# An attention and mixture-of-experts kernel: all queue lists laid out anew, and the idle products taken out

## The chip, the core and the metric

The kernel runs on one core of a Trainium2 chip. The metric is the device time of one execution in microseconds. The kernel before took 829.53 us (median of 3 runs, 828.97 to 829.89).

## The reference, cut to what matters

32 sequences (here called tiles) of 128 tokens with 256 features each go through two blocks. Everything is fp32.

```
A (cross-attention), 16 heads of 16:
  q = layernorm(x) Wq' + bq;  k, v = ctx Wk' + bk, ctx Wv' + bv
  x = x + tanh(g_xattn) * (softmax(where(mask, -1e9, q k' / 4)) v Wo' + bo)
B (causal self-attention and experts) on y = layernorm(x):
  q, k from rope(y), v from y; causal softmax; attn_out with out_proj
  u = layernorm(y + attn_out) * ln1_w + ln1_b
  gates = softmax(u gate_w' + gate_b); the two largest of 8 experts are kept
  moe = sum over the chosen experts of gate * (u expert_w' + expert_b)
  x = x + tanh(g_ffn) * (layernorm(u + moe) * ln2_w + ln2_b)
```

## The kernel before, in words

A tile is 128 tokens by 256 features. Weights stay in SBUF, each as a high and a low part (`w_Aka`, `w_Akb` and so on); a product of fp32 accuracy is three products of the parts, high by high, high by low and low by high (`products`, L391 to L396). A part is made by ScalarE (`split_high`, L746; a copy) and VectorE (`split_low`, L929; a subtraction). Activations are split in the same way (`high_part`, L752, L758, on ScalarE; `low_part`, L967, L974, on VectorE).

Eight banks of PSUM are used: four score banks hold the 16 heads' 128 by 128 scores, and four work banks hold everything else. Which use takes which work bank, and in which turn, is written out in `WORK_USES`; `take_work` (L386) makes TensorE wait for the reader of the use before.

One attention of one tile goes through the score banks thus:

1. ScalarE seeds the four banks with the mask (`seed_scores`, L765, L776; 4 instructions).
2. TensorE adds the scores, query by key (`scores`, L505, 16 products at L516).
3. VectorE takes the negative maxima, bank by bank (`maxima`, L1017, L1022; 4 instructions), and `max_parts` (L1026) makes a bf16 high and low part of them, four copies of 2 x 16 columns.
4. For A, ScalarE seeds the banks with the transposed mask (`seed_scores_t`, L779, L785). TensorE writes the scores again, key by query (`scores_t`, L521, 32 products at L535).
5. TensorE transposes the maxima (`transpose_max`, L546), ScalarE copies them out (`max_transposed`, L818), and TensorE adds them with `pick`, a table with a row for each of 16 heads (`subtract_max`, L556, 16 products).
6. ScalarE takes the exponentials (`exponentials`, L826; 4 instructions); for B, GpSimd zeroes what is not causal (`causal`, L1343). TensorE multiplies by the values (`attend`, L574); ScalarE copies the result to `o_raw` (`raw_values`, L834), one buffer for A and B.

Then follow a transposition (L585), the division by the sums (VectorE), another transposition, the split, and the output projection (`project_o`). Around this stand the norms: VectorE has statistics (L952, L960) and the scaling (L964), GpSimd the inverse root (`inverse_root`, L1260, L1263). GpSimd also splits the context (`context_parts`, L1271, L1273) and widens the mask (`mask_of_tile`, L1280). It waits for a tile's context and mask with one semaphore, `ld_c`.

**The order of the work** is written out by hand. Each engine has a list, run once for each round r, and each entry names its own tile by an offset, as `scores("A", 2 * r - 1)`. An entry whose tile does not exist is left out (`live`). A round has two tiles, and each queue is strictly in order, so the lists are the schedule: TensorE L627 to L741, ScalarE L858, VectorE L1141, GpSimd L1389, and SyncE, which only issues transfers, L342 to L382. In TensorE's list A runs two tiles ahead of B and five ahead of the experts (`expert_pair`, L613). A tile's k and q projections are made for two tiles together (`project_pair`, L455).

In the first rounds and the last ones few entries are live. There `keep_busy` (L407) issues products of the identity that nobody reads:

```python
            def keep_busy(use, t, count):
                bank = take_work(use, t)
                for _ in range(count):
                    pe.matmul(bank[:], ident_bf[:], ident_bf[:].unsqueeze(1).to_broadcast([P, GROUP, P]), start=True, stop=True)
```

SyncE's list before the rounds loads tiles 0 and 1 first, then Ak, Av, tile 2's x and context, Aq, small rows, tile 3, and so on. The rows of the norms, the gates and the expert biases (11 transfers) come behind.

## Time and profile before

| What | before |
|---|---|
| median of 3 runs | 829.53 us (828.97 to 829.89) |
| span of the profiled execution | 829.5 us |
| TensorE busy | 779.7 us (94%) |
| VectorE busy | 667.5 us (80%) |
| ScalarE busy | 564.4 us (68%) |
| GpSimd busy | 473.0 us (57%) |
| products of `keep_busy` | 167 |

The profile gives the time from the first to the last instruction (the span), and for each engine the time in which one of its instructions ran. A busy TensorE is not TensorE at its peak, since products overlap and their ends are modelled; the time from one start to the next says more. "Idle before, releaser" is the time that an engine had nothing to run, and the instruction that ended it. PEclk is the granted TensorE clock as a share of 2.4 GHz.

### The profile page before, as it was taken

The numbers are of one execution on the slowest core, as the hardware profiler recorded it, in microseconds if no ns is written. First come the engines' busy times: TensorE is split into PE (matmuls) and PEld (weight loads), VectorE is DVE, ScalarE is ACT, GpSimd is POOL, SyncE is SP. The second block draws the span as 40 slices with busy tenths as digits, with TensorE's granted clock in tenths as the row PEclk, the third lists the DMA queues.
The fourth block names the chain that finished last, engine by engine and source line by source line (L and its number), as shares of the span: only waits on it lengthen the run. The fifth ranks groups of instructions, "written<-read, shape, count | busy, mean of one in ns | idle before, by whom it ended". The sixth has DMA issues, their size and how long they took to land.

```text
span 829.5 us, 24325 instructions
## 1 busy us (share of the span) xinstructions
PE 779.7 (94%) x9515; PEld 611.9 (74%) x9515; DVE 667.5 (80%) x1908; ACT 564.4 (68%) x1268; POOL 473.0 (57%) x854
## 2 busy tenths in 40 slices
PE   8888989999999999999999999999999999999896
PEld 4465768777787787778787788778778777777663
DVE  5756668797978979797988979797988979787876
ACT  5786767777786777777776777678677777764320
POOL 8434535566665646566574646566564655555343
PEclk9999999999999999999999999999999999999999
DMA  7510000010100101010100101010010000000000
GB/s 202 159 39 16 2 17 16 8 37 9 37 8 2 37 8 36 9 36 9 29 16 2 38 8 37 8 37 9 10 35 2 9 8 8 9 8 8 8 7 20
DMA packets 33570, 20.75 MB, mean 25 GB/s; under 512 B 11672, under 2 KB 33456, under 8 KB 33456
## 3 DMA queue, kind: packets, MB, share of 16 engines
q1 hardware_dynamic: 33456, 19.19, 8.1%
q8 instruction: 76, 1.25, 0.6%
q14 instruction: 38, 0.31, 0.1%
HBM read 14.99 MB, written 4.19 MB: 23 GB/s over the span
## 4 chain that ended last, share of the span: by engine, by line
PE 56%; ACT 24%; DVE 14%; issue 4%; POOL 1%; DMA 0%; SPq 0%; DVEq 0%; POOLq 0%
PE bank L395 26%; PE bank L516 8%; PE bank L535 7%; ACT bank L776 6%; DVE neg_max_A L1022 6%; ACT bank L785 5%; DVE moe L1131 4%; ACT probs_B L826 3%; PE bank L556 3%; PE bank L585 3%; ACT probs_A L826 3%; PE bank L574 2%; PE bank L404 2%; ACT k_heads_B L809 2%; PE bank L546 1%
## 5 line engine op out<-in xcount | busy, mean ns | idle before, releaser
L1343 POOL TENSOR_SCALAR_AFFINE_SELECT probs_B<-probs_B 128x512 f32<-128x512 f32 x128 | 77.3, 640 | 184.4 <-ACT probs_B L826 184.4
L1131 DVE SCALAR_TENSOR_TENSOR moe<-bank,gates,moe 128x256 f32<-128x256 f32 x256 | 123.2, 481 | 48.2 <-PE bank L395 33.2
L785 ACT ACTIVATE bank<-mask_add 128x512 f32<-128x512 bf16 x128 | 76.6, 602 | 49.2 <-DVE neg_max_A L1022 49.2
L395 PE MATMUL bank<-w_expertsa,u_t_a 128*128 128x512 f32 x256 | 105.6, 413 | 0.1
L395 PE MATMUL bank<-w_expertsa,u_t_b 128*128 128x512 f32 x256 | 100.9, 394 | 0.0
L395 PE MATMUL bank<-w_expertsb,u_t_a 128*128 128x512 f32 x256 | 100.9, 394 | 0.0
L1022 DVE TENSOR_REDUCE neg_max_A<-bank 128x4 f32<-128x512 f32 x128 | 79.5, 684 | 11.9 <-PE bank L516 11.5
L1022 DVE TENSOR_REDUCE neg_max_B<-bank 128x4 f32<-128x512 f32 x128 | 79.3, 682 | 5.5 <-PE bank L516 5.5
L776 ACT ACTIVATE bank<-mask_add 128x512 f32<-128x512 bf16 x128 | 69.8, 626 | 0.0
L776 ACT ACTIVATE bank<-causal_add 128x512 f32<-128x512 bf16 x128 | 69.7, 623 | 0.0
L826 ACT ACTIVATE probs_A<-bank 128x512 f32<-128x512 f32 x128 | 66.1, 603 | 4.4 <-PE bank L556 2.2
L826 ACT ACTIVATE probs_B<-bank 128x512 f32<-128x512 f32 x128 | 66.2, 607 | 3.2 <-PE bank L556 1.1
L834 ACT ACTIVATE o_raw<-bank 128x512 f32<-128x512 f32 x64 | 38.5, 602 | 27.8 <-PE bank L574 27.8
L395 PEld LDWEIGHTS bank<-w_expertsa,u_t_a 128*128 128x128 f32 x256 | 49.1, 192 | 10.6 <-issue 0.4
L1260 POOL TENSOR_SCALAR var_eps<-mean_var 128x1 f32<-128x1 f32 x64 | 12.3, 192 | 77.7 <-DVE mean_var L960 75.2
L395 PEld LDWEIGHTS bank<-w_expertsa,u_t_b 128*128 128x128 f32 x256 | 48.1, 188 | 11.4
L395 PEld LDWEIGHTS bank<-w_expertsb,u_t_a 128*128 128x128 f32 x256 | 48.3, 189 | 6.7
L535 PEld LDWEIGHTS bank<-q_heads_A,k_heads_A 32*128 32x128 f32 x1024 | 31.4, 186 | 22.4 <-ACT bank L785 22.4
L809 ACT ACTIVATE k_heads_A<-bank,k_cols_A,head_rows 128x256 f32<-128x256 f32 x64 | 30.9, 565 | 23.0 <-PE bank L395 23.0
L535 PE MATMUL bank<-q_heads_A,k_heads_A 32*128 32x128 f32 x1024 | 37.5, 283 | 8.1 <-ACT bank L785 7.4
L411 PE MATMUL bank<-ident_bf 128*128 128x512 bf16 x167 | 42.7, 396 | 1.9 <-ACT k_heads_B L809 1.9
L516 PE MATMUL bank<-k_heads_A,q_heads_A 32*128 32x256 f32 x512 | 36.7, 399 | 5.8 <-ACT bank L776 4.7
(224 smaller groups left out, 2440.5 us busy)
## 6 DMA issues: line engine op xcount, KB each, us to landing
x_in<-in_x SPq DMA_DIRECT2D x32, 128.0 KB, 2.2
ctx_t<-in_ctxT SPq DMA_DIRECT2D x32, 128.0 KB, 2.2
out<-y_out SPq DMA_DIRECT2D x32, 128.0 KB, 1.7
w_stage<-in_expertsT SPq DMA_DIRECT2D x8, 256.0 KB, 4.3
mask_u<-in_masks SPq DMA_DIRECT2D x32, 32.0 KB, 2.1
w_stage<-in_in_projT SPq DMA_DIRECT2D x3, 256.0 KB, 4.8
w_stage<-in_WkT SPq DMA_DIRECT2D x1, 256.0 KB, 3.5
w_stage<-in_WvT SPq DMA_DIRECT2D x1, 256.0 KB, 3.6
```

The costliest lines, as they stand in the source:

```text
L395: done = pe.matmul(out_ap, l, r, start=n == 0, stop=n == len(terms) - 1)
L411: pe.matmul(bank[:], ident_bf[:], ident_bf[:].unsqueeze(1).to_broadcast([P, GROUP, P]), start=True, stop=True)
L516: done = pe.matmul(score_banks[g][:, c * 2 * P:(c + 1) * 2 * P], queries[strip, half, c, :], keys[strip, half, c, :, :], start=False, stop ...
L535: pe.matmul(score_banks[g][:, i * P:(i + 1) * P], keys[strip, half, c, odd, :], queries[strip, half, c, :], start=tag == "B" and i == 0, s ...
L776: act.activation(score_banks[g][:].rearrange("p (h k) -> p h k", k=P), mask[:, 0:1, :].to_broadcast([P, GROUP, P]), ACT.Copy).then_inc(sem ...
L785: act.activation(score_banks[g][:].rearrange("p (h k) -> p h k", k=P), mask_add[t % MASK_SLOTS][:, 1:2, :].to_broadcast([P, GROUP, P]), AC ...
L809: act.activation(k_heads[tag][pair % PAIR_SLOTS][:, :, c, odd, :], bank[:, c * PAIR * P:(c + 1) * PAIR * P].rearrange("p (j n) -> p j n", ...
L826: act.activation(probs[tag][:, g * GROUP:(g + 1) * GROUP, :].rearrange("p h q -> p (h q)"), score_banks[g][:], ACT.Exp, scale=SCALE).then_ ...
L834: act.activation(o_raw[:], work_bank(tag + "_values", t)[:], ACT.Copy).then_inc(sem[tag + "_or"], 1)
L1022: dve.tensor_reduce(neg_max[tag][:, g * GROUP:(g + 1) * GROUP], score_banks[g][:].rearrange("p (h k) -> p h k", k=P), AXIS_X, ALU.max, neg ...
L1131: dve.scalar_tensor_tensor(out=moe[(e + 1) % 2][:], in0=bank[:, (e % 2) * EMBED:(e % 2 + 1) * EMBED], scalar=gates[:, e:e + 1], in1=moe[e ...
L1343: pool.affine_select(out=part, in_=part, compare_op=ALU.is_ge, fill=0.0, base=0, pattern=[[0, GROUP], [1, P]], channel_multiplier=-1).then ...
```

## The change

- `PIECES = 4`: what was a loop over four score banks is now a list entry for each piece of one bank. `scores` and `subtract_max` increment their semaphore once, behind the last product, where they did it four times; `scores_t` now increments one.
- Every engine's list and `WORK_USES` are new. A still runs two tiles ahead of B and five ahead of the experts.
- SyncE's list before the rounds is gone: each transfer stands in a round.
- All `keep_busy` entries are gone.
- `pick` has 4 columns of rows instead of 16 (`GROUP` instead of `HEADS`), is made by VectorE from the identity, and `max_parts` writes each head's maximum once, 16 columns per part where it was 64. GpSimd's `make_picks` (a memset and two selects of 128x2048) goes.
- `o_raw` has a buffer for A and one for B. Some waits that another wait implies go, others are added.

```diff
-        pick = sb("pick", [P, HEADS, P], BF16)
+        pick = sb("pick", [P, GROUP, P], BF16)
+        strip_rows = sb("strip_rows", [P, GROUP])
-        o_raw = sb("o_raw", [P, BANK])
+        o_raw = {t: sb(f"o_raw_{t}", [P, BANK]) for t in "AB"}
+        def score_piece(c):
+            return scores_ps[:, c * PIECE_BANKS:(c + 1) * PIECE_BANKS, :].rearrange("p g (h k) -> p (g h) k", k=P)
...
-                        if c == CHUNKS - 1:
-                            done.then_inc(sem[tag + "_s"], 1)
+                done.then_inc(sem[tag + "_s"], 1)
...
-                hi, lo = copies[:, :, 0:HEADS], copies[:, :, HEADS:2 * HEADS]
-                whole = neg_max[tag][:].unsqueeze(1).to_broadcast([P, GROUPS, HEADS])
+                hi, lo = copies[:, :, 0:GROUP], copies[:, :, GROUP:2 * GROUP]
+                whole = neg_max[tag][:].rearrange("p (g n) -> p g n", n=GROUP)
...
+            def exponentials(tag, c, t):
+                if not live(t):
+                    return
+                act.wait_ge(sem[tag + "_sm"], t + 1)
+                act.activation(probs[tag][:, c * PIECE_HEADS:(c + 1) * PIECE_HEADS, :], score_piece(c), ACT.Exp,
+                               scale=SCALE).then_inc(sem[tag + "_exp"], 1)
```

SyncE's new list, with its waits inside `load_weight` and `load_tile` as before:

```python
            for r in rounds:
                store(2 * r - 30)
                if r == 13: load_weight("E2")
                if r == 11: load_weight("E1")
                load_tile(2 * r - 19)
                if r == 10: load_weight("Bk")
                if r == 1:  load_weight("Ao"); load_row(bo_A)
                store(2 * r - 29)
                if r == 1:  load_weight("Ak")
                if r == 13: load_weight("E7")
                if r == 10: load_weight("Bq"); rope_cos, rope_sin, bv_B
                if r == 3:  load_weight("Av")
                if r == 14: load_weight("E6")
                if r == 11: load_weight("Bv")
                if r == 10: load_weight("Bo"); bo_B, ln1_w, ln1_b, ln2_w, ln2_b, gate_bias, bias_f x3, gate_f
                if r == 12: load_weight("E5"); load_weight("E3")
                load_tile(2 * r - 18)
                if r == 12: load_weight("E4")
                if r == 11: load_weight("E0")
                if r == 0:  load_weight("Aq"); head_rows, bias_cols, two gains, bv_A
```

TensorE's new list (each line in the order of the list):

```
transpose_max B 2r-5, o_transposed A 2r-3, y_transposed 2r-5, subtract_max B 2r-5, normalise B 2r-6,
project_o A 2r-3, project_v_a 2r-2, project_v_b 2r-5, gate 2r-7, o_transposed B 2r-6, rope_transposed 2r-4,
x_t 2r, scores A 2r-2, attend B 2r-5, rope_transposed 2r-3, project_o B 2r-6, normalise B 2r-5,
project_k_b r-2, transpose_max A 2r-2, scores_t A 2r-2, subtract_max A 2r-2, expert_pair 0 2r-7,
transpose_gates 2r-7, project_q_b r-2, expert_bias_sum 2r-7, expert_pair 1 and 2 2r-7, scores B 2r-4,
attend A 2r-2, o_transposed B 2r-5, y_transposed 2r-4, expert_pair 3 2r-7, u_transposed 2r-6,
scores_t B 2r-4, transpose_max B 2r-4, normalise A 2r-2, subtract_max B 2r-4, gate 2r-6, project_v_b 2r-4,
o_transposed A 2r-2, project_o B 2r-5, expert_pair 0 2r-6, project_v_a 2r-1, project_o A 2r-2,
transpose_gates 2r-6, scores A 2r-1, attend B 2r-4, expert_bias_sum 2r-6, expert_pair 1 2r-6, x_t 2r+1,
transpose_max A 2r-1, scores_t A 2r-1, subtract_max A 2r-1, expert_pair 2 and 3 2r-6, project_k_a r,
scores B 2r-3, attend A 2r-1, project_q_a r, normalise A 2r-1, u_transposed 2r-5, scores_t B 2r-3
```

The stretches of the other lists that the prediction speaks of:

```
ScalarE: ... seed_scores A pieces 2, 3 2r-9, gates_transposed 2r-14, seed_scores_t 0 2r-9, raw_values B 2r-12,
  seed_scores_t 1, 2, 3 2r-9, max_transposed A 2r-9, high_x 2r-7, exponentials A 0, 1, 2 2r-9, seed_scores B 0, 1 2r-11, ...
  keep_keys A r-4, raw_values A 2r-9, keep_queries A r-4, ... seed_scores A 0 to 3 2r-8 ...
  (in ScalarE's list 2r-9 is the odd tile of A, 2r-1 in TensorE's, and 2r-12 the even tile of B, 2r-4 in TensorE's)
VectorE: ... statistics A 2r-1, statistics 2, low_o A, apply_x 2r-2, ... add_values A 2r-4, ... low_x 2r-2,
  maxima A 0, 1, 2 2r-4, low_rope 2r-5, maxima A 3 2r-4, max_parts A 2r-4 ...
GpSimd:  scale_shift_u 2r-12, base_a 2r-8, causal 0 to 2, context_parts 2r-4, causal 3, inverse_root 2, base_a 2r-7,
  mask_of_tile 2r-6, inverse_root 1, inverse_root B, rope, ... inverse_root A 2r-4, ... mask_of_tile 2r-5, ...
```

## Rows read from the trace of the kernel before

**Rows 1.** Windows over two stretches: start and end, length, busy us of PE, PEld, DVE, ACT, POOL, PEclk.

```profile
16.20:118.80 102.60, 89.88 (x1142) 62.19 (x1142) 63.91 (x147) 74.52 (x159) 46.39 (x84) 1.00 0.20 57
118.80:731.90 613.10, 593.78 (x7594) 482.00 (x7594) 524.10 (x1530) 448.75 (x1017) 367.13 (x666) 1.00 0.06 17
```

**Rows 2.** Timeline of PE over one round: start, length, line, operation, idle before.

```profile
353.25 1.08 PE L574 MATMUL bank<-probs_B,values_B 128*32 128x128 f32 x32
354.61 1.15 PE L516 MATMUL bank<-k_heads_A,q_heads_A 32*128 32x256 f32 x16 [0.27 <-ACT bank L776]
...
371.14 1.17 PE L535 MATMUL bank<-q_heads_B,k_heads_B 32*128 32x128 f32 x32
372.25 0.23 PE L546 MATMUL bank<-ident_bf,neg_max_bf_B 128*128 128x128 bf16 x1
...
378.46 1.15 PE L516 MATMUL bank<-k_heads_A,q_heads_A 32*128 32x256 f32 x16
379.53 1.08 PE L574 MATMUL bank<-probs_B,values_B 128*32 128x128 f32 x32
...
381.94 0.40 PE L395 MATMUL bank<-w_expertsa,u_t_b 128*128 128x512 f32 x1
382.79 1.17 PE L535 MATMUL bank<-q_heads_A,k_heads_A 32*128 32x128 f32 x32 [0.46 <-ACT bank L785]
```

**Rows 3.** Timeline of PE, the start of the next round.

```profile
401.76 0.50 PE L516 MATMUL bank<-k_heads_A,q_heads_A 32*128 32x256 f32 x4 [0.28 <-ACT bank L776]
```

**Rows 4.** Timelines of DVE and ACT in the same round.

```profile
379.62 2.48 DVE L1022 TENSOR_REDUCE neg_max_A<-bank 128x4 f32<-128x512 f32 x4 [0.46 <-PE bank L516]
382.48 0.18 DVE L1034 CAST neg_max_bf_A<-neg_max_A 128x64 bf16<-128x64 f32 x1
...
380.35 2.39 ACT L785 ACTIVATE bank<-mask_add 128x512 f32<-128x512 bf16 x4 [1.50 <-DVE neg_max_A L1022]
382.68 0.58 ACT L834 ACTIVATE o_raw<-bank 128x512 f32<-128x512 f32 x1
...
397.50 2.07 ACT L826 ACTIVATE probs_B<-bank 128x512 f32<-128x512 f32 x4
399.43 2.18 ACT L776 ACTIVATE bank<-mask_add 128x512 f32<-128x512 bf16 x4
```

**Rows 5.** Timeline of SP, the transfers' issues.

```profile
0.79 0.37 SPq L313 DMA_DIRECT2D x_in<-in_x  x1
...
17.68 1.09 SPq L309 DMA_DIRECT2D gate_bias<-in_L_ffn_gate_b  x1
...
21.35 1.23 SPq L313 DMA_DIRECT2D x_in<-in_x  x1
```

**Rows 6.** Timelines of POOL and ACT, the first instructions behind a transfer.

```profile
4.14 0.40 POOL L1271 CAST ctx_ab_a<-ctx_t 128x256 fp32r<-128x256 f32 x1 [1.79 <-DMA mask_u<-in_masks]
4.62 0.73 POOL L1273 TENSOR_TENSOR ctx_ab_b<-ctx_t,ctx_ab_a 128x256 fp32r<-128x256 f32 x1
...
9.50 0.63 ACT L750 ACTIVATE w_Aqa<-w_stage 128x512 fp32r<-128x512 f32 x1 [0.75 <-DMA w_stage<-in_WqT]
```

**Rows 7.** Timeline of PE, the scores of A for tiles 0 and 1.

```profile
16.19 1.15 PE L516 MATMUL bank<-k_heads_A,q_heads_A 32*128 32x256 f32 x16 [0.27 <-ACT q_heads_A L795]
31.27 1.15 PE L516 MATMUL bank<-k_heads_A,q_heads_A 32*128 32x256 f32 x16 [0.38 <-ACT bank L776]
```

**Rows 8.** Timeline of PE, the scores of B for tiles 30 and 31.

```profile
765.45 1.15 PE L516 MATMUL bank<-k_heads_B,q_heads_B 32*128 32x256 f32 x16
783.84 1.15 PE L516 MATMUL bank<-k_heads_B,q_heads_B 32*128 32x256 f32 x16
```

**Rows 9.** PE where the clock fell: a window of 3.4 us, and a group of 32 products in it.

```profile
748.10:751.50 3.40, 3.40 (x54) 2.64 (x50) 2.43 (x14) 1.55 (x6) 0.00 (x0) 0.50 0.00 0
...
747.85 1.93 PE L535 MATMUL bank<-q_heads_B,k_heads_B 32*128 32x128 f32 x32 [1.27 <-DVE neg_max_B L1022]
```

**Rows 10.** Window of PE, products of `keep_busy` (L411) alone: length, busy us of PE, of PEld.

```profile
16.20:118.80 102.60, 25.88 (x108) 9.68 (x108) 1.00 0.20 57
```

More of the change, by code:

```diff
@@ L534, in scores_t @@
                             i = 2 * c + odd
[L535 to L537 removed]
+                            done = pe.matmul(scores_ps[:, g, i * P:(i + 1) * P], keys[strip, half, c, odd, :],
+                                             queries[strip, half, c, :], start=tag == "B" and i == 0, stop=False,
+                                             skip_group_check=True)
+                done.then_inc(sem[tag + "_st"], 1)
             def transpose_max(tag, t):
@@ new lines, in tensor_program @@
+                project_o("A", 2 * r - 3)
+                project_v_a(2 * r - 2)
+                project_v_b(2 * r - 5)
+                gate(2 * r - 7)
+                o_transposed("B", 2 * r - 6)
+                rope_transposed(2 * r - 4)
+                x_t(2 * r)
+                scores("A", 2 * r - 2)
+                attend("B", 2 * r - 5)
+                rope_transposed(2 * r - 3)
+                project_o("B", 2 * r - 6)
+                normalise("B", 2 * r - 5)
+                project_k_b(r - 2)
@@ new lines, in tensor_program @@
+                transpose_max("A", 2 * r - 2)
+                scores_t("A", 2 * r - 2)
+                subtract_max("A", 2 * r - 2)
+                expert_pair(0, 2 * r - 7)
+                transpose_gates(2 * r - 7)
+                project_q_b(r - 2)
+                expert_bias_sum(2 * r - 7)
+                expert_pair(1, 2 * r - 7)
+                expert_pair(2, 2 * r - 7)
+                scores("B", 2 * r - 4)
+                attend("A", 2 * r - 2)
+                o_transposed("B", 2 * r - 5)
@@ L628, in tensor_program @@
+                y_transposed(2 * r - 4)
+                expert_pair(3, 2 * r - 7)
+                u_transposed(2 * r - 6)
+                scores_t("B", 2 * r - 4)
+                transpose_max("B", 2 * r - 4)
+                normalise("A", 2 * r - 2)
+                subtract_max("B", 2 * r - 4)
                 gate(2 * r - 6)
                 project_v_b(2 * r - 4)
-                if r == 1:
-                    keep_busy("x_t", 2, 3)
+                o_transposed("A", 2 * r - 2)
+                project_o("B", 2 * r - 5)
@@ L650, in tensor_program @@
-                scores_t("A", 2 * r - 1)
-                transpose_max("A", 2 * r - 1)
-                rope_transposed(2 * r - 2)
-                subtract_max("A", 2 * r - 1)
-                normalise("B", 2 * r - 4)
                 expert_pair(3, 2 * r - 6)
-                o_transposed("B", 2 * r - 4)
-                if r == 1:
-                    keep_busy("A_v", 2, 4)
+                project_k_a(r)
+                scores("B", 2 * r - 3)
                 attend("A", 2 * r - 1)
+                project_q_a(r)
@@ L726, in tensor_program @@
-                y_transposed(2 * r - 2)
-                scores("B", 2 * r - 2)
-                if r == 0:
-                    keep_busy("x_t", 2, 4)
-                attend("A", 2 * r)
-                o_transposed("B", 2 * r - 3)
-                project_v_a(2 * r + 1)
-                normalise("A", 2 * r)
-                if r == 16:
-                    keep_busy("B_values", 30, 9)
-                scores_t("B", 2 * r - 2)
-                transpose_max("B", 2 * r - 2)
-                if r == 0:
-                    keep_busy("x_t", 2, 5)
@@ L1299, in rope, with keep @@
                 pool.tensor_tensor(roped[:], roped[:], rope_tmp[:], ALU.add).then_inc(sem["rope3"], 1)
+            def keep(t):
+                if not live(t):
+                    return
+                if t == 0:
+                    pool.wait_ge(sem["c_fold_2"], 2)
+                kept = x1[t % X1_SLOTS]
+                pool.tensor_tensor(kept[:], kept[:], rows["ln2_b"][:], ALU.add).then_inc(sem["kept"], 1)
             def finish(t):
```

1031 lines of the change are left out of this document (535 added, 496 removed).

## The prediction

> **What bounds the kernel now.** I read the windows by stage first. From tile 5's scores of A at 118.8 us to tile 31's at 731.9 TensorE is busy for 593.78 of 613.10 us [rows 1]; no other engine comes near. These are 26 tiles or 13 rounds, so a round is 47.16 us; two starts of the same entry, 354.61 and 401.76, give 47.15 [rows 2, 3]. Around this steady stage stand a fill of 118.8 us and a drain of 829.5 - 731.9 = 97.6 us. Of the fill, 16.2 us pass before the first scores [rows 7], 102.6 us between them and the sixth.
>
> The timeline shows what TensorE's steady round still loses. The ends of its products are modelled, so I take start to start. An entry that waits for nothing starts just before the modelled end of the one ahead (378.46 + 1.15 = 379.61, next start 379.53) [rows 2]. Against that 353.25 + 1.08 leads to a start at 354.61 (about 0.35 us late, the seeds), and the last expert product, started at 381.94 and usually 0.23 apart, is followed by `scores_t` only at 382.79: 0.85 us, 0.64 of it lost, again to ScalarE's seeds [rows 2]. Both bounds of the whole loss: the empty time is (613.10 - 593.78) / 13 = 1.5 us a round [rows 1]; summing every late start in the round as above I get 2.5. So the round can fall to 44.65 us at the best, and nothing but other waits decides where it lands: the products in it are the same ones. That is worth at most 2.5 x 13 = 32 us.
>
> The sum is made against the span of the profiled execution, 829.5 us, which is the median of the runs too. About 0.2% (1.7 us) is what a measurement of this kernel can tell from no change.
>
> **Part 1, the steady round: -13 us.** Pieces of one bank are the same instructions as before, of the same 512 columns; they cost nothing and only let other work stand between them. I walk through the new lists with the lengths of before. The cycle of the score banks is: scores 1.15, maxima 2.4, one more seed 0.6, `scores_t` 1.17, subtraction, four exponentials 1.93, four seeds 2.1 [rows 2, 4].
>
> - Odd tile of A: TensorE puts attend B, the bias, one expert pair and `x_t` between `scores` and `scores_t`, about 4.0 us. ScalarE's chain is: scores and first maximum 1.95, seed 0.6, then `raw_values` B 0.55, which now stands between pieces 0 and 1, then three seeds 1.8: 5.05 us [rows 4]. A wait of 1.05 us, where before it was 0.64. This is the largest that I find.
> - `transpose_max` A now stands ahead of `scores_t`. At the even tile 5.2 us of work cover it; then ScalarE's copy of the maxima hides behind `scores_t` and the subtraction no longer waits. This takes away some 0.6 us a round in both halves.
> - Odd B to even A: between the subtraction and `scores` stand 4.2 us of TensorE work against 1.93 + 2.18 us of ScalarE's [rows 4]: a wait of 0.2 in place of 0.35.
> - Even A to even B: keys, four exponentials, a copy of the gates, queries and four seeds on ScalarE come to 12.8 us, as much as TensorE has: 0.1. At the rope transposition GpSimd's chain fits within 0.1.
>
> The waits left add up to about 1.5 of 2.5 us, so I take 1.0 us off a round, 13 us in all; bounds 0 (the new wait grows by what the others give) and 32. The narrower `max_parts` saves part of a cast of 0.18 us [rows 4] and its partner, but the transposition behind it has work ahead of it: nothing. The smaller `pick` frees GpSimd in a stretch in which nothing waits for it: nothing. A second `o_raw` removes no wait that the trace shows: nothing.
>
> Four increments become one in `scores` and `subtract_max`. The trace shows no tail for them: behind four increments the next start is 0.08 us before the group's end, behind none (371.14 + 1.17, next 372.25) 0.06, and VectorE starts at 379.62, with the group's end at 379.61 [rows 2, 4]. I take nothing. The Trainium skill, page "TensorE: Matmul & The Clock Gate", section "The cost: per-tile semaphore tail", gives 26.3 ns for each increment; ten fewer a tile would be an estimated 8.4 us, and the sum by it 817.7. No row here bears that out.
>
> **Part 2, the start: +10.2 us.** SyncE's order changes most. Tile 0 now comes behind Aq, five small transfers, Ao, its row, Ak and Av, and tile 2 behind 32 transfers, among them all rows of the norms and gates. The new lists need tile 2 early: TensorE has `x_t` of tile 2 ahead of the scores of tile 0, and GpSimd has `context_parts` of tile 2 ahead of `mask_of_tile` 0, without which tile 0's seeds can't start. One issue takes (17.68 - 0.79) / 34 = 0.497 us, and the five small ones from 17.68 take 3.67 us up to 21.35 [rows 5]. Tile 2's mask has 34 transfers ahead of it, 29 plain and 5 small: 0.8 + 29 x 0.497 + 3.67 = 18.9 us at its issue. From issue to the first user a mask took 2.5 us (1.68 to 4.14) and a weight 3.8 (5.70 to 9.50) [rows 6]; the rings are full here, so I take 3.5: 22.4. Then context parts 1.2, mask 0.4, four seeds 2.2 and 0.2 of handing on: 26.4 us, against 16.2 [rows 4, 6, 7]. Bounds 25 and 28.5. What this hides: the splits of the weights, both first transpositions and the first k and q products.
>
> **Part 3, the first five tiles: +1.9 us.** From tile 0 to tile 1 the chain (scores, maxima, seeds, `scores_t`, exponentials, attend, two transpositions, output projection) took 15.1 us [rows 7]. ScalarE no longer has four weight splits of 0.6 us ahead of `max_transposed`, and the next seeds stand ahead of the high part: 13.4. By the same walk all five steps come to 97.8 us against 102.6: -4.8. But the 108 idle products of this stage held 25.88 of 89.88 busy us [rows 1, 10], and without them the clock will fall at times. What that costs is seen in the drain: there the granted clock was 0.50 for 3.4 us, that is 1.2 GHz, where TensorE had stood idle for 1.27 us at a stretch, and 32 products took 1.93 us, not 1.17 [rows 2, 9]. The A chain has about 5 us of products a tile. With half of them slow in tiles 0 to 2, less later, I get 2.5 + 1.5 + 1.5 + 0.7 + 0.5 = +6.7. Bounds 3 and 15.
>
> **Part 4, the drain: -2.5 us.** B of tile 31 started 18.4 us behind B of tile 30 [rows 8], since normalise and `o_transposed` of tile 30 stood between; now only attend and two expert pairs do: 15. With 1.9 us ahead of tile 30's and 2.7 behind tile 31's (fewer idle products in the way) the walk gives -7.9. A walk forgets waits, so I take half, -4, and put +1.5 for a slow clock. Bounds -9 and +4.
>
> Sum: 829.5 - 13 + 10.2 + 1.9 - 2.5 = **826.1 us**.
>
> **The rivals.**
> 1. *The seeds keep the round where it is.* Place: ScalarE's odd tile, where `raw_values` now stands inside the seeds. If TensorE waits there, and at VectorE's maxima (`low_rope` stands ahead of the fourth), for over 2 us a round, part 1 falls to about 0.2 x 13 = 2.6 us. Then fill losses decide: 826.1 + 10.4 = **836.5**, slower. It decides from a round of 46.9 us on. For it: VectorE is busy for 524 of 613 us [rows 1], so it has little to catch up with. Against it: each engine's stretch between two scores fits by my walk.
> 2. *The clock.* The fill and the drain run mostly at 1.2 GHz. The real products of the fill's stage are 89.88 - 25.88 = 64 busy us; if 12 us more of them turn slow on the chain, **838**. For it: the idle products end, in the trace, just where the next wait ends. Against it: from tile 3 on the real products alone fill most of the time. The Trainium skill's same page, "HAM oscillation — how this bites in real kernels", says that a product stream broken by waits falls back to the low clock and starts cold again each time; by that rule this rival would be the likelier. The trace agrees where it shows the low clock, after 748 us.
> 3. *The search nearly reaches the floor.* A round of 45.0 us: 826.1 - 15 = **811**. For it: the lists were rewritten entry by entry; against it: the 1.05 us wait.
> 4. *The change does less than it says at the semaphores' end, or more.* If each of the 128 groups with fewer increments ends 0.02 us sooner (0.08 against 0.06 above), 2.6 us: **823.5**; by the page named in part 1 more.
>
> **How the numbers follow.** Chances: forecast 0.43, rival 1 0.24, rival 2 0.15, rival 3 0.14, rival 4 0.04. The forecast's own range is 819 to 832. Faster than 827.9: 0.33 of the forecast's 0.43, all of rivals 3 and 4, and 0.03 of the others: 0.54. Within 0.2%: 0.07 of the forecast and 0.03 of rival 1: 0.10. Slower: 0.36. The range 810 to 840 takes in rivals 1 to 3 and the bounds of the fill, and leaves under 2 in 10 outside.
>
> **What would show it.** In the changed profile: scores of tile 0 at 25 to 28.5 us, first idle time ended by transfers of tile 2's mask or x; two starts of an even tile's scores 46.1 us apart; idle time ahead of L535's successor in odd tiles, ended by ScalarE's seeds, near 1 us; a clock of 0.50 in some windows up to 60 us; scores of tile 5 near 131. The prediction is wrong if the round is under 45.5 or over 46.8, if the first scores come before 22 us, or if the clock stays at 1.00 up to 100 us.

## The result, and the profile after

| What | before | after |
|---|---|---|
| median | 829.71 us (828.97 to 829.95, 4 runs) | 856.93 us (856.15 to 857.54, 4 runs) |
| ratio, 95% interval | | 1.0329 (1.0314 to 1.0344) |
| span of the profiled execution | 829.5 us | 855.7 us |
| VectorE busy | 667.5 us | 685.7 us |
| TensorE busy | 779.7 us | 753.5 us |

The kernel became 3.3% slower; the forecast was 826.1 us, with a range up to 840. Two executions, one of the kernel before at 1049.64 us and one of `best1` at 4024.16, are left out as disturbed. Beside the experiments the kernel before took 829.1 to 831.0 us, and each ratio is to the runs taken with it. The first view is the windows of the changed kernel by stage: first scores of A to the sixth, sixth to the last, the end, and a stretch of the fill. Columns as in [rows 1].

```profile
26.99:136.40 109.41, 80.33 (x1012) 64.60 (x1011) 58.18 (x146) 72.55 (x157) 42.17 (x77) 0.81 0.10 29
136.40:758.30 621.90, 589.86 (x7595) 486.71 (x7594) 544.09 (x1528) 440.60 (x1013) 369.12 (x664) 1.00 0.06 17
758.30:855.70 97.40, 74.08 (x712) 57.29 (x711) 72.34 (x212) 31.91 (x78) 46.86 (x81) 0.95 0.03 11
27.50:44.00 16.50, 10.59 (x118) 7.97 (x111) 6.99 (x15) 10.84 (x21) 3.01 (x6) 0.50 0.27 83
```

Two things are to be seen. The clock was 0.81 in the first steps where it had been 1.00, and 0.50 between 27.5 and 44 us. And in the steady stage VectorE is busy for 544.09 us with 1528 instructions, where it was 524.10 us with 1530 [rows 1]: 1.5 us more a round for the same work. The 26.2 us of span divide so:

| Stage | before | after | difference | forecast |
|---|---|---|---|---|
| to the first scores | 16.2 | 27.0 | +10.8 | +10.2 |
| first five steps | 102.6 | 109.4 | +6.8 | +1.9 |
| 26 steady tiles | 613.1 | 621.9 | +8.8 | -13 |
| the end | 97.6 | 97.4 | -0.2 | -2.5 |

The start, in the timelines of SP, POOL, ACT and PE:

```profile
17.24 0.47 SPq L327 DMA_DIRECT2D mask_u<-in_masks  x1
...
22.26 0.87 POOL L1336 CAST ctx_ab_a<-ctx_t 128x256 fp32r<-128x256 f32 x1 [6.46 <-DMA mask_u<-in_masks]
23.21 1.05 POOL L1338 TENSOR_TENSOR ctx_ab_b<-ctx_t,ctx_ab_a 128x256 fp32r<-128x256 f32 x1
24.34 0.41 POOL L1343 TENSOR_SCALAR mask_add<-mask_u 128x256 bf16<-128x256 uint8 x1
...
24.78 2.15 ACT L759 ACTIVATE scores_ps<-mask_add 128x512 f32<-128x512 bf16 x4 [2.30 <-POOL mask_add L1343]
...
26.99 0.81 PE L533 MATMUL scores_ps<-k_heads_A,q_heads_A 32*128 32x256 f32 x4
```

This is the forecast's chain: tile 2's mask, its context parts, the mask of tile 0, four seeds. Its terms are not the forecast's: the mask was issued at 17.24 (forecast 18.9) and took 5.0 us to its first user (3.5), and the context parts and the mask took 2.5 us (1.6). The context parts are slow themselves, 0.87 and 1.05 us where tile 1's took 0.40 and 0.73 in this trace (13.68 and 14.16): VectorE makes the low parts of Bk and Bq at the same time, from 22.22 to 23.68. And the 2.30 us of ACT's wait show that without it the seeds would only have stood there 2.3 us sooner; something else was next in line.

The steady round: late entries in PE's timeline. From 471.52 to 519.55 is one round, 48.03 us, where it was 47.15 [rows 2, 3].

```profile
471.52 1.15 PE L533 MATMUL scores_ps<-k_heads_A,q_heads_A 32*128 32x256 f32 x16
...
476.15 0.23 PE L560 MATMUL bank<-ident_bf,neg_max_bf_A 128*128 128x128 bf16 x1 [0.54 <-DVE neg_max_bf_A L1071]
476.41 1.17 PE L550 MATMUL scores_ps<-q_heads_A,k_heads_A 32*128 32x128 f32 x32
...
488.56 0.30 PE L424 MATMUL bank<-ident,o_norm_A 128*128 128x128 f32 x1 [0.53 <-DVE u_t_b L989]
...
496.50 0.33 PE L424 MATMUL bank<-ident,roped 128*128 128x128 f32 x1 [0.61 <-POOL roped L1364]
...
517.74 0.39 PE L415 MATMUL bank<-w_Ava,ctx_ab_a 128*128 128x256 f32 x1 [0.75 <-DVE values_B L1051]
...
519.55 0.50 PE L533 MATMUL scores_ps<-k_heads_A,q_heads_A 32*128 32x256 f32 x4
```

Counted as in the prediction, start against start, these are 0.70, 0.60 (with 0.19 at the entry ahead of it), 0.68 and 0.91 us late, and the whole loss is 3.4 us a round (48.03 less the 44.65 that the prediction took as the floor) against 2.5. Of the four ends of waits, three are VectorE's. What VectorE and GpSimd did ahead of two of them:

```profile
486.40 0.26 DVE L1078 RECIPROCAL inv_sum_A<-bank 128x16 f32<-128x16 f32 x1 [0.43 <-PE bank L597]
486.58 0.49 DVE L1069 CAST neg_max_bf_B<-neg_max_B 128x16 bf16<-128x16 f32 x1
487.10 0.65 DVE L1071 TENSOR_TENSOR neg_max_bf_B<-neg_max_B,neg_max_bf_B 128x16 bf16<-128x16 f32 x1
487.67 0.41 DVE L1086 TENSOR_TENSOR o_norm_A<-bank,inv_sum_A 128x256 f32<-128x256 f32 x1
...
498.44 0.17 DVE L1069 CAST neg_max_bf_A<-neg_max_A 128x16 bf16<-128x16 f32 x1
...
498.75 0.22 DVE L1125 TENSOR_TENSOR beats<-logits 128x64 f32<-128x64 f32 x1
...
499.39 0.22 DVE L1130 TENSOR_TENSOR beats<-beats,equals 128x64 f32<-128x64 f32 x1
...
514.74 0.60 DVE L1125 TENSOR_TENSOR beats<-logits 128x64 f32<-128x64 f32 x1
515.26 0.66 DVE L1126 TENSOR_TENSOR equals<-logits 128x64 f32<-128x64 f32 x1
515.96 0.32 DVE L1128 TENSOR_TENSOR equals<-equals,lower_tri 128x64 f32<-128x64 f32 x1
516.31 0.79 DVE L1130 TENSOR_TENSOR beats<-beats,equals 128x64 f32<-128x64 f32 x1
517.13 0.22 DVE L1132 TENSOR_REDUCE rank<-beats 128x8 f32<-128x64 f32 x1
...
486.31 0.73 POOL L1382 TENSOR_TENSOR y_out<-v_n,x 128x256 f32<-128x256 f32 x1
486.99 0.73 POOL L1404 TENSOR_TENSOR base_B<-yn,row_bo_B 128x256 f32<-128x256 f32 x1
...
514.03 1.82 POOL L1419 TENSOR_SCALAR_AFFINE_SELECT probs_B<-probs_B 128x512 f32<-128x512 f32 x3 [5.12 <-ACT probs_B L808]
515.80 0.40 POOL L1336 CAST ctx_ab_a<-ctx_t 128x256 fp32r<-128x256 f32 x1
516.28 0.74 POOL L1338 TENSOR_TENSOR ctx_ab_b<-ctx_t,ctx_ab_a 128x256 fp32r<-128x256 f32 x1
517.08 0.64 POOL L1419 TENSOR_SCALAR_AFFINE_SELECT probs_B<-probs_B 128x512 f32<-128x512 f32 x1
```

The same small instruction takes 0.22 us with GpSimd at rest (499.39) and 0.79 us beside GpSimd (516.31); the cast of the maxima 0.17 (498.44) and 0.49 (486.58). `o_norm_A`, which reads a bank, keeps its 0.41, and `rank`, with one input in SBUF, keeps its 0.22 (517.13) inside GpSimd's instruction from 517.08. Long ones end just behind the end of a GpSimd instruction: 487.07 behind 487.04, 487.75 behind 487.72, 516.28 behind 516.20, 517.10 behind 517.02. What VectorE pays is the rest of GpSimd's instruction, not a factor on its own.

### The profile page after: what moved, and what is told of

Its sections match the earlier page's. It is cut to its first block, busy times and chain, and to the rows that moved or that the text cites. A ratio compares the mean times of both kernels' runs of the same rounds, so it can differ in the third digit from the quotient of the medians.

```text
span 855.7 us, 23886 instructions
## 1 busy us (share of the span) xinstructions
PE 753.5 (88%) x9348; PEld 615.4 (72%) x9348; DVE 685.7 (80%) x1912; ACT 555.5 (65%) x1268; POOL 468.6 (55%) x851
## 4 chain that ended last, share of the span: by engine, by line
DVE 42%; PE 33%; POOL 10%; issue 7%; ACT 5%; DMA 1%; SPq 1%; DVEq 0%; POOLq 0%
PE bank L415 16%; DVE moe L1170 7%; DVE neg_max_A L1058 5%; DVE neg_max_B L1058 4%; PE scores_ps L550 4%; PE scores_ps L533 3%; PE bank L586 3%; PE bank L597 2%; POOL rstd L1328 2%; POOL rope_tmp L1360 2%; PE bank L424 2%; DVE beats L1130 2%; DVE x L1095 1%; POOL roped L1364 1%; POOL roped L1358 1%
## 5 line engine op out<-in xcount | busy, mean ns | idle before, releaser
L1058 DVE TENSOR_REDUCE neg_max_B<-scores_ps 128x4 f32<-128x512 f32 x128 | 79.2, 680 | 18.1 <-PE scores_ps L533 17.9
L766 ACT ACTIVATE scores_ps<-mask_add 128x512 f32<-128x512 bf16 x128 | 70.5, 594 | 31.2 <-DVE neg_max_A L1058 31.2
L1058 DVE TENSOR_REDUCE neg_max_A<-scores_ps 128x4 f32<-128x512 f32 x128 | 80.6, 682 | 3.1 <-PE scores_ps L533 2.5
L808 ACT ACTIVATE probs_A<-scores_ps 128x512 f32<-128x512 f32 x128 | 71.7, 607 | 16.6 <-PE scores_ps L572 16.6
L808 ACT ACTIVATE probs_B<-scores_ps 128x512 f32<-128x512 f32 x128 | 69.8, 602 | 8.5 <-PE scores_ps L572 8.5
L759 ACT ACTIVATE scores_ps<-mask_add 128x512 f32<-128x512 bf16 x128 | 72.6, 619 | 2.3 <-POOL mask_add L1343 2.3
L759 ACT ACTIVATE scores_ps<-causal_add 128x512 f32<-128x512 bf16 x128 | 72.6, 617 | 0.0
L415 PEld LDWEIGHTS bank<-w_expertsb,u_t_a 128*128 128x128 f32 x256 | 48.3, 189 | 6.8
L533 PE MATMUL scores_ps<-k_heads_B,q_heads_B 32*128 32x256 f32 x512 | 37.9, 411 | 9.8 <-ACT scores_ps L759 9.8
L1395 POOL TENSOR_TENSOR base_A<-x_in,row_bo_A 128x256 f32<-128x256 f32 x32 | 24.8, 776 | 33.2 <-DVE x L1095 33.1
L550 PE MATMUL scores_ps<-q_heads_B,k_heads_B 32*128 32x128 f32 x1024 | 38.6, 288 | 2.8 <-DVE neg_max_B L1058 2.8
L550 PE MATMUL scores_ps<-q_heads_A,k_heads_A 32*128 32x128 f32 x1024 | 40.0, 296 | 0.6 <-ACT scores_ps L766 0.2
```

What stands on the lines that cost most here:

```text
L415: done = pe.matmul(out_ap, l, r, start=n == 0, stop=n == len(terms) - 1)
L533: done = pe.matmul(scores_ps[:, g, c * 2 * P:(c + 1) * 2 * P], queries[strip, half, c, :], keys[strip, half, c, :, :], start=False, stop=T ...
L550: done = pe.matmul(scores_ps[:, g, i * P:(i + 1) * P], keys[strip, half, c, odd, :], queries[strip, half, c, :], start=tag == "B" and i == ...
L759: act.activation(score_piece(c), mask[:, 0:1, :].to_broadcast([P, PIECE_HEADS, P]), ACT.Copy).then_inc(sem[tag + "_seed"], 1)
L766: act.activation(score_piece(c), mask_add[t % MASK_SLOTS][:, 1:2, :].to_broadcast([P, PIECE_HEADS, P]), ACT.Copy).then_inc(sem["A_seed_t"], 1)
L808: act.activation(probs[tag][:, c * PIECE_HEADS:(c + 1) * PIECE_HEADS, :], score_piece(c), ACT.Exp, scale=SCALE).then_inc(sem[tag + "_exp"], 1)
```

## The experiments

The theory after the result: VectorE's list sets the steady round, because two stretches of it stand beside GpSimd instructions; the start and the low clock account for the rest. The rival for the round was ScalarE's seeds. "The changed kernel" is the one of the result; the profiles give the round as the distance of two starts of an even tile's scores.

### The start and the clock

**The kernel before without its idle products.** All its `keep_busy` entries are deleted.

> The kernel before without its idle products, nothing else changed. Theory that the clock costs what the changed kernel shows in its first steps (6.8 us, of which the low clock is to explain most): 829.5 + 5 to 8 us, first scores still at 16, the granted clock at 0.50 in several windows before 120 us, and the steady round unchanged at 47.15. Rival, that the idle products are mostly in the way (a walk gave 4.8 us for the order without them): within 2 us of before. If the steady round too gets longer without them, both are wrong.

846.5 us (842.3 to 848.7; ratio 1.0189, 1.0149 to 1.0228). The windows by stage:

```profile
18.90:127.30 108.40, 79.65 (x1034) 63.10 (x1035) 62.64 (x147) 74.92 (x159) 41.79 (x78) 0.80 0.19 46
127.30:740.20 612.90, 593.70 (x7590) 482.30 (x7591) 523.73 (x1530) 448.36 (x1016) 366.52 (x666) 1.00 0.06 17
740.20:842.90 102.70, 80.49 (x686) 61.91 (x686) 72.11 (x214) 32.24 (x80) 46.81 (x80) 0.89 0.03 10
```

The steps cost 5.8 us more (102.6 before), as expected; but the start costs 2.7 and the end 5.1 as well, and the clock is 0.89 there. The idle products were worth 13.4 us of span in the profiled executions (15.5 us between the medians); the forecast had allowed 8.2 (6.7 and 1.5). The end of the changed kernel, without idle products too, takes 97.4 us against 102.7 here. How much of these 5.3 us is the new order stays open: the clock was 0.95 there and 0.89 here, and TensorE's busy time, 74.08 and 80.49 us, differs by more than the span.

**The changed kernel with idle products in the fill.**

```diff
+                if r == 1:
+                    keep_busy("A_max_t", 0, 13)
                 transpose_max("A", 2 * r - 2)
...
```

> The changed kernel with some 130 idle products put where TensorE waits between the scores of tiles 0 and 5. If the low clock is what made its first five steps 6.8 us longer than in the kernel before: the five steps fall from 109.4 to 102 to 104 us and the time to 850 to 852. If the new order itself is slower in the fill, they stay above 108 and the time at 855 or more. The steady round stays at 48.0 in both.

848.2 us (846.95 to 849.27; ratio 1.0209, 1.0194 to 1.0224). The window of the five steps:

```profile
27.50:128.60 101.10, 89.79 (x1120) 63.65 (x1119) 57.72 (x146) 72.51 (x157) 41.80 (x76) 1.00 0.12 32
```

109.4 became 101.1 at a clock of 1.00, a little below the expectation: the low clock costs 8.3 us here. With idle products in both, the new order is worth 1.5 us against the 102.6 of before; without them in either it loses 1.0 (109.4 against the 108.4 above). So the order of the fill gives little or nothing.

**The changed kernel with the old order of the transfers** (SyncE's list of before in place of the new one), and then with three entries moved as well (in GpSimd's list `key_bias`, in ScalarE's `tanh_of_gains`, in VectorE's the low parts of Av and Aq, all behind the first norm).

> The changed kernel with the old order of the transfers. Theory that the start is set by tile 2's mask behind 34 transfers: first scores at 17 to 19 us in place of 27.0, the time 856.9 - 8 to 10 = 847 to 849, all later distances between scores as in the changed kernel. Rival, that the new lists of the other engines need the late start for other reasons (key and query projections, the splits): first scores not before 24 us, 854 or more.

> The changed kernel with the old order of the transfers and three entries moved behind the first norm: GpSimd's key_bias (waits for bias_cols until 9.9 us), ScalarE's tanh_of_gains (until 10.4 us) and VectorE's low parts of Av and Aq. If these entries hold the start: first scores at 17.5 to 20 us, where the old transfers alone gave 24.8. If the projections at the low clock do: 22 us or later.

854.35 us (852.33 to 855.21), first scores at 24.85; then 851.65 (one run), first scores at 24.29. Both theories miss, and both times the other case came. The transfers are 2.2 of the 10.8 us. VectorE's first xn came at 9.67 in place of 14.22, so the three entries did hold the first norm, but two things were next. One is TensorE's pace: the 24 products of the k and q projections start 0.21 us apart (15.85 to 20.90), where in `best3`, below, with idle products ahead of them, it is 0.12 (13.45 to 16.26), 2.3 us in all; the granted clock reads 1.00 in both stretches and doesn't show it. The other is ScalarE's list. Its timeline with the three entries moved:

```profile
13.78 0.63 ACT L695 ACTIVATE w_Aoa<-w_stage 128x512 fp32r<-128x512 f32 x1 [3.93 <-DMA w_stage<-in_WoT]
14.31 0.36 ACT L705 ACTIVATE xn_t_a<-bank 128x256 fp32r<-128x256 f32 x1
...
15.98 0.63 ACT L695 ACTIVATE w_Bka<-w_stage 128x512 fp32r<-128x512 f32 x1 [1.21 <-DMA w_stage<-in_in_projT]
16.69 0.63 ACT L695 ACTIVATE w_Bqa<-w_stage 128x512 fp32r<-128x512 f32 x1
17.23 0.36 ACT L705 ACTIVATE xn_t_a<-bank 128x256 fp32r<-128x256 f32 x1
```

The split of Ao stands ahead of the first high part of x, those of Bk and Bq ahead of the second. The new lists fit the new order of transfers, in which these weights come early. A transfer list and the lists of its readers have to be changed together.

### The parts costed at nothing

**The kernel before with the narrow table, 16 columns of maxima and single increments**, its lists unchanged:

```diff
-                        if c == CHUNKS - 1:
-                            done.then_inc(sem[tag + "_s"], 1)
+                done.then_inc(sem[tag + "_s"], 1)
```

> The kernel before, its lists as they were, with the narrow table of rows, 16 columns for each part of the maxima and one increment for scores and subtract_max where there were four. The prediction costed all of it at nothing: within 1.5 us of 829.5, round 47.15. Rival 4 of the prediction: each of the 128 groups ends 0.02 us sooner, 827; by the Trainium skill's 26.3 ns for each increment 821.

832.36 us (10 runs) against 830.96; ratio 1.0017 (1.0007 to 1.0028). There is no gain; the 26 steady tiles take 614.6 us where they took 613.1, the round 47.26 in place of 47.15. Rival 4 falls. The Trainium skill, "TensorE: Matmul & The Clock Gate", "The cost: per-tile semaphore tail", gives 26.3 ns for each increment; twelve fewer a tile would be an estimated 10 us less, and what was measured is 1.4 us more. Which of the three edits costs that little was not tried.

### VectorE's list in the steady round

Four single moves and a first combination:

```diff
 after_rank
-                gate_rank(2 * r - 10)
                 add_values("B", 2 * r - 8)
                 low_o("A", 2 * r - 6)
+                gate_rank(2 * r - 10)
 after_max_parts
+                max_parts("B", 2 * r - 7)
                 inverse_sums("A", 2 * r - 5)
-                max_parts("B", 2 * r - 7)
                 normalise("A", 2 * r - 5)
 after_stats (both lines go behind gate_choice(2 * r - 10))
-                statistics("2", 2 * r - 11)
-                mean_variance("2", 2 * r - 11)
```

`after_base`, the fourth, moves `base_b(2 * r - 9)` of GpSimd's list behind `inverse_root("1", 2 * r - 10)`. `after_steady` has the moves of `after_max_parts`, `after_stats` and `after_base`, and `apply_v` ahead of `gates_low`.

> The changed kernel; in VectorE's list gate_rank of the even tile stands behind the addition of the values of B and the low part of A's output, no longer ahead of them. Theory that the steady round is 48.0 us because VectorE's list is late there (gate_rank takes 2.6 us beside two GpSimd instructions, and the projection of A's values waits 0.91 us for the bank that the addition behind it frees): that wait goes, the round falls by 0.5 to 0.9 us, the time by 6 to 12. Rival, that ScalarE's seeds hold the round (rival 1 of the prediction): no change of the round, the wait moves on.

> The changed kernel; in GpSimd's list base_b of the odd tile stands behind context_parts and two inverse roots, which wait for nothing. Theory that GpSimd's 3.84 us of waiting at that entry make VectorE idle (1.04 and 0.44 us at 503 to 504) and the last maxima of a round late: round -0.2 to -0.6 us. If VectorE has time to catch up before its next dated work, the round stays at 48.0.

> The changed kernel; in VectorE's list max_parts of B's odd tile stands ahead of inverse_sums A, no longer between it and normalise A. There the two parts take 0.49 and 0.65 us beside GpSimd's y_out and base_B, and o_transposed of A is 0.60 us late. Theory that the steady round is set by VectorE's list: the parts start 0.6 us sooner, the 0.60 us go to 0 to 0.2, and the round falls to 47.4 to 47.7. Rival, that later waits take it back: o_transposed on time and the round still 48.0.

> The changed kernel; the statistics of the last norm of the odd tile (0.43 and 0.18 us) stand behind gate_choice in VectorE's list, no longer ahead of the normalisation of A and gate_rank. Where moving gate_rank itself took 0.91 us from the projection of A's values and gave 1.36 to the transposition of the gates, this move lets both start 0.5 us sooner. If VectorE's list sets the round: 47.5 or below. If the last norm is then late for GpSimd and the store: 48.0 or above.

> The changed kernel with three moves at once: max_parts of B ahead of inverse_sums A, the statistics of the last norm behind gate_choice, and base_b of the odd tile behind the inverse roots with the scaling of the last norm ahead of gates_low. If the steady round is set by VectorE's list and its collisions: 46.8 to 47.3, time 838 to 848. If it is set elsewhere: 47.8 to 48.1 and 854 or more.

| run | time | steady round |
|---|---|---|
| changed kernel | 856.93 us | 48.0 |
| after_rank | 860.11 (2 runs) | 48.3 |
| after_base | 857.83 (2 runs) | 48.05 |
| after_max_parts | 846.88 (1 run) | 47.15 |
| after_stats | 855.49 (1 run) | 48.0 |
| after_steady | 854.53 (2 runs) | 47.15 |

`after_steady` has the expected round but not the expected time: its end takes 102.8 us (853.2 - 750.4), where that of `after_max_parts` takes 96.3. The same 712 products keep TensorE busy for 78.1 us there against 72.8, at a granted clock of 0.91 against 0.97, so the clock is in this difference; whether the other moves brought it about was not tried. `after_base` only passed GpSimd's wait on: 3.36 us at the inverse root behind it. In `after_max_parts` one entry moved by one place is worth 10 us. VectorE, then TensorE, in `after_max_parts`:

```profile
480.78 0.17 DVE L1069 CAST neg_max_bf_B<-neg_max_B 128x16 bf16<-128x16 f32 x1
480.99 0.17 DVE L1071 TENSOR_TENSOR neg_max_bf_B<-neg_max_B,neg_max_bf_B 128x16 bf16<-128x16 f32 x1
481.21 0.26 DVE L1078 RECIPROCAL inv_sum_A<-bank 128x16 f32<-128x16 f32 x1
481.50 0.42 DVE L1086 TENSOR_TENSOR o_norm_A<-bank,inv_sum_A 128x256 f32<-128x256 f32 x1
481.92 0.42 DVE L989 TENSOR_TENSOR u_t_b<-bank,u_t_a 128x256 fp32r<-128x256 f32 x1
...
482.42 0.23 PE L560 MATMUL bank<-ident_bf,neg_max_bf_B 128*128 128x128 bf16 x1
482.49 0.30 PE L424 MATMUL bank<-ident,o_norm_A 128*128 128x128 f32 x1
```

The two parts take 0.17 each and fill the gap in which VectorE waited for TensorE; the 0.60 and the 0.19 us are gone, and the round is that of before. This one move does two things at once, it fills a gap and leaves GpSimd's neighbourhood: VectorE's busy time in the steady stage falls from 544.1 to 539.3 us, 0.37 us a round, which is less than half of the 0.85. `after_stats` and `after_rank` handed the 0.91 us on: the transposition of the gates now waits,

```profile
521.34 0.30 PE L618 MATMUL bank<-ident,gates 128*128 128x128 f32 x1 [1.20 <-DVE values_A L1051]
```

in `after_rank`, for the addition of A's values, which frees its bank and stands behind the moved entries. The next run puts the statistics behind that too (and keeps the move of `max_parts`):

> The changed kernel with max_parts of B ahead of inverse_sums A and, new, the last norm's statistics behind the addition of A's values, which frees the bank that the transposition of the gates takes. If the steady round is VectorE's list and nothing else: both the 0.60 and the 0.91 us of waiting go, round 46.1 to 46.5, time 833 to 837. Rival, that the 0.91 us are handed on once more: 47.15 and 846.

851.75 us (850.34 to 853.15), round 47.35: a miss, worse than `after_max_parts` alone. The gates are still 0.3 us late, `transpose_max` of A, 0.70 late before, is now 0.94, and `x_t` waits 0.41 us for ScalarE's `raw_values` B (469.31 to 469.95), which stands inside the seeds as rival 1 had it. In the changed kernel VectorE never idles from 504.6 to 519.9 us: an entry moved inside that stretch only chooses who waits. What must shrink is the stretch. Fewer collisions alone are no gain either: in `after_rank` VectorE is busy for 532.3 us of the steady stage, 11.8 less than in the changed kernel, and the round is longer. (That `bias_sum` stands ahead of `max_parts` of A, 0.41 us on the way to the 0.70, was not tried otherwise: the transposed maxima take the bank that it reads.)

### Is it the collision, or GpSimd's own list?

> The changed kernel without the 128 GpSimd instructions that zero what is not causal (attend of B waits for the exponentials instead), so that GpSimd is free for about 184 us more. It leaves out the causal part of B's attention behind the maxima. Theory that VectorE's instructions on SBUF are slower beside GpSimd's and that this sets the steady round: round at 47.0 or below, gate_rank's five instructions back at 1.1 to 1.3 us. Rival, that the collisions are harmless: gate_rank gets short and the round stays within 0.3 us of 48.0.

> The kernel before without the same 128 instructions: the counterpart. If the lists of before already keep the two engines apart, its round falls by less than that of the changed kernel: by 0.2 us or less from 47.15. If both fall by the same, collisions don't tell the two kernels apart.

> The changed kernel with each of GpSimd's 128 causal instructions cut to one head of four; the order, the waits and the counts stay. It leaves out the causal part for three heads of four. It tells the length of GpSimd's work from the place of its entries. If it is the time that GpSimd spends beside VectorE: round 46.7 to 47.0, as without these instructions. If GpSimd's standing at the exponentials ahead of its other entries did it: round near 48.0.

Each was run once. Without the 128 instructions the round of the changed kernel falls from 48.0 to 46.7 (840.05 us), that of the kernel before stays at 47.15 (829.65 us). With the instructions cut to a quarter it is 46.7 too (839.93 us), so GpSimd's standing at the exponentials costs nothing; the length does. (GpSimd's busy time falls by 77.6 us, from 468.6; the 184 us of the expectation are what it waited at these entries in the kernel before.) VectorE's busy time in the steady stage falls from 544.1 to 524.3 us, that of before; in the kernel before it hardly moves, from 524.1 to 522.2. VectorE in one round of each, the changed kernel first and then the one without the 128 instructions:

```profile
471.52:519.55 48.03, 45.39 (x585) 37.44 (x585) 42.18 (x119) 33.90 (x78) 28.86 (x52) 1.00 0.07 20
```

```profile
461.00:507.70 46.70, 45.11 (x588) 37.51 (x587) 40.55 (x119) 33.93 (x78) 23.98 (x44) 1.00 0.07 20
```

Its 119 instructions take 1.6 us less, and the five of `gate_rank` are 0.23, 0.22, 0.23, 0.22, 0.22. These runs still make GpSimd's list shorter. The cleaner one leaves all work as it is and, on top of `after_max_parts`, moves one entry of GpSimd's list:

```diff
                 causal(2, 2 * r - 10)
-                context_parts(2 * r - 4)
                 causal(3, 2 * r - 10)
...
                 inverse_root("1", 2 * r - 11)
+                context_parts(2 * r - 4)
```

> after_max_parts with one more move: GpSimd's context_parts of the even tile stands behind the inverse roots, out of the stretch in which VectorE runs gate_rank. All work stays. If VectorE is slowed by what GpSimd does at that time: gate_rank 2.6 us down to 1.6 to 2.1, the wait of the projection of A's values down from 0.91 by as much, round 47.15 - 0.4 to 0.8. If only the last causal instruction or the place in VectorE's list counts: round within 0.15 us of 47.15. A loss would mean that a later norm collides with context_parts in its new place.

838.95 us (one run), round 46.63. VectorE and GpSimd:

```profile
503.53 0.67 DVE L1126 TENSOR_TENSOR equals<-logits 128x64 f32<-128x64 f32 x1
504.23 0.23 DVE L1128 TENSOR_TENSOR equals<-equals,lower_tri 128x64 f32<-128x64 f32 x1
504.49 0.23 DVE L1130 TENSOR_TENSOR beats<-beats,equals 128x64 f32<-128x64 f32 x1
...
502.29 1.83 POOL L1419 TENSOR_SCALAR_AFFINE_SELECT probs_B<-probs_B 128x512 f32<-128x512 f32 x3 [5.12 <-ACT probs_B L808]
```

GpSimd ends at 504.12; from there on VectorE's instructions are short again. `gate_rank` takes 2.0 us in place of 2.6, and the projection of A's values is 0.27 us late in place of 0.91. The move also lets the last causal instruction start sooner, but nothing waited for it in the changed kernel: its attend of B follows the scores 1.08 us behind their start, without a wait (472.60).

### All together

`best1`, `best2` and `best3` put the findings together: the move of `max_parts`, the old transfers, the three entries, the idle products of the fill and 17 or 18 ahead of the first scores; `best1` also has 13 in the drain and the move of the statistics, `best2` has ScalarE's splits of Ao, Bk and Bq moved instead, `best3` the move of `context_parts` on top.

> Everything together: the two moves in VectorE's list, the old order of the transfers with the three entries moved, the idle products of the fill and some at the start and in the drain. If the causes add up: start -8, first steps -8, steady round -1.7 a round, so 857 - 38 = 815 to 822, faster than the kernel before. If they overlap (an earlier start meets later transfers): 825 to 835.

> after_max_parts with the old order of the transfers, the three entries of after_start moved, ScalarE's splits of Ao, Bk and Bq behind the first two high parts of x, and the idle products of the fill. If the splits ahead of the norms are what held the start: first scores at 17 to 20 us; with 101 us for the first five steps, 612.6 for the steady tiles and 96 for the end 827 to 831 us, about as fast as the kernel before. If the start is held by the first products at the low clock: first scores at 22 or later, 833 to 837.

> best2 with the move of context_parts of after_context, and the split of Ao behind the second high part of x as well. If the causes add up: steady round 46.63 in place of 47.15, so 13 x 0.5 = 7 us less than best2, and the start 1 to 2 us sooner: 825.5 to 828.5 us, faster than the kernel before (829.2) by 0.1 to 0.4%. If the earlier start or the idle products collide with the move: 830 or more.

| run | time | ratio to before, 95% interval | first scores |
|---|---|---|---|
| best1 | 841.00 us | 1.0145 (1.0123 to 1.0167) | 23.8 |
| best2 | 835.48 us | 1.0074 (1.0060 to 1.0088) | 22.5 |
| best3 | 827.32 us | 0.9971 (0.9959 to 0.9983) | 22.3 |

`best1` missed, for the round (47.35) and the start; `best2` came out as its second case. `best3` is inside its expectation, though its start came only 0.2 us sooner. `best3` is 0.3% faster than the kernel before. Its windows, from a profiled execution of 829.7 us, the slowest of its seven runs:

```profile
22.33:125.90 103.57, 92.49 (x1123) 64.59 (x1123) 57.78 (x146) 72.33 (x157) 38.94 (x70) 0.97 0.16 44
125.90:732.10 606.20, 588.38 (x7591) 485.72 (x7590) 532.37 (x1528) 440.28 (x1013) 370.17 (x666) 1.00 0.06 18
```

Its steady stage takes 606.2 us, 6.9 less than before, at a round of 46.63. Its start is still 6 us later than that of before. The trace shows what stands there next: the split of Bk waits for its transfer until 16.29, that of Bq follows, and only at 17.55 does ScalarE copy the keys, whose products ended at 15.12. Whether moving these splits again brings the start back was not tried.

## Why the prediction was wrong

The forecast missed the span by 29.6 us (855.7 against 826.1): 21.8 in the steady round, 4.9 in the first steps, 2.3 at the end, 0.6 at the start.

- **Part 1 is the step that failed**: "I walk through the new lists with the lengths of before". The largest wait that the walk found, 1.05 us at the odd tile of A, is there with 0.70: `scores_t` starts at 476.41, when ScalarE's seeds are out (476.36) and `max_parts` is through (476.09) with its transposition. What was left out are 0.79 us at the transpositions behind `max_parts` B, 0.91 at the projection of A's values and 0.68 at the rope: together 2.4, and 3.4 - 2.4 leaves 1.0, with the 0.70 in it, where the forecast said 1.5. The walk followed TensorE and ScalarE and took VectorE as able to keep up. But a length of before holds only for what runs beside it, and VectorE's instructions took 1.5 us a round more. So the steady stage grew by 8.8 us where -13 was forecast. The experiments show 0.85 us of the round to be the place of `max_parts` (in part a gap that it fills), and 0.52 that of `context_parts`; with GpSimd's causal instructions gone or short, 1.3 go. With both moved the round is 46.63, near the 46.15; the rope's 0.69 us remain.
- "The narrower `max_parts` saves part of a cast: nothing" was right about its sum and blind to its place: narrow or not, 0.49 and 0.65 us beside GpSimd.
- **Rival 1** said that the round stays at 46.9 or more, with 836.5. Its effect came, its mechanism did not: `raw_values` inside the seeds was not what took the gains, and shows only as 0.41 us in `after_two_moves`. Its argument for, VectorE busy for 524 of 613 us, was the right row, read too lightly.
- **The rule that I did not weigh**: the Trainium skill, "SBUF — State Buffer", "SBUF: two separate sides", says that VectorE and GpSimd share a pair of ports as an exclusive lock, taken by whichever starts first, for VectorE instructions in a two-port mode, or with two SBUF inputs against a GpSimd instruction that reads SBUF. The trace agrees (0.22 to 0.79 us, with the end just behind GpSimd's; the reader of a bank and `rank` unchanged). It spoke against new lists for both engines and belonged among the rivals.
- **Part 2** was right in its chain, and in its sum (+10.2 against +10.8) partly by luck: the issue came 1.7 us sooner than forecast and the transfer took 1.5 us longer, which cancel. No run shows that the rings were full; the trace gives 5.0 us from issue to first user where 3.5 was taken. The runs show that a second limit stood 2.2 us behind the chain: the entries ahead of the first norm, the slow pace of the first projections, and the weight splits of the lists. "What this hides" named splits and products, and gave them no price.
- **Part 3**: the mis-sized terms are both. The order gave 1.5 us at most (with idle products; -1.0 without) and not 4.8, the clock took 8.3 and not 6.7. Here too the walk was too good, by 3 to 6 us.
- **Part 4**: the sum was 0.2 against 2.5 us of gain, and its two terms can't be told apart. Ends of kernels with the new lists and no idle products in the drain took 94.8 us at a clock of 0.99 (`after_start`), 97.4 at 0.95, and 102.8 at 0.91 (`after_steady`); the kernel before without its idle products took 102.7 at 0.89. So the clock is worth several us, more than the 1.5 that was read from one window [rows 9], and how much the order gives stays open.
- **Rival 2** had the right kind of cost: a granted clock of 0.81 over 109 us, and 8.3 us. The Trainium skill, "TensorE: Matmul & The Clock Gate", "HAM oscillation — how this bites in real kernels", says that a stream of products broken by waits falls back to the low clock. The trace agrees in the fill, with 0.50 from 27.5 to 44 us.

## What to carry to other kernels

When the order of an engine's list changes, ask for each short VectorE instruction that reads SBUF what GpSimd does at that moment, and take its length from a row with the same neighbour: it may have to sit out GpSimd's instruction. A wait that one move removes belongs to a stretch: look who is next in that stretch before counting it as a gain. Idle products are priced by running the kernel without them, not by one window.

## What was unexpected

- One entry of VectorE's list moved by one place (two instructions of 0.17 us) gave 10 us of 857.
- 13.4 us of span (15.5 between the medians) hang on 167 products that nobody reads.
- Small instructions suffer most beside GpSimd: 0.22 us became 0.79, while a wait of GpSimd itself, 3.84 us at `base_b`, could be passed on to another entry without a change of the round.
